# Products of adj_hi first in each half block, four slots of split blocks, eight raw half blocks

## The reference

```
x = layernorm(x + relu(adj @ x @ K + b))            # pass 0
v0 = x, then five applications of adj, each with a three-layer perceptron:
    v = mlp(adj @ u, uv);  u = mlp(adj @ v, vu);  ...   # passes 1 to 5
mlp(x, W1..3, b1..3): leaky_relu(leaky_relu(leaky_relu(x@W1+b1)@W2+b2)@W3+b3), slope 0.01
out = layernorm(x + v)                               # after pass 5
```

## Time and profile before

| | |
|---|---|
| median of three runs | 1184.89 us |
| the profiled execution | 1184.28 us |
| its span, first to last instruction | 1182.5 us |
| mean granted clock of TensorE | 0.997 |
| PE busy | 1157.3 us, 98% |
| DVE busy | 738.1 us, 62% |
| ACT busy | 661.8 us, 56% |
| DMA, mean rate over the span | 221 GB/s |

### The profile page before, as it was taken

How to read it: one execution, slowest core, us unless ns; L and a number is a source line. 1 busy time by engine, 2 the same in 40 slices (tenths; PEclk the granted TensorE clock), 3 DMA queues, 4 the chain that set the end, 5 groups by cost and what they waited for, 6 DMA issues and landing times.

```text
span 1182.5 us, 13669 instructions
## 1 busy us (share of the span) xinstructions
PE 1157.3 (98%) x5220; PEld 951.0 (80%) x5220; DVE 738.1 (62%) x885; ACT 661.8 (56%) x815; POOL 0.2 (0%) x4
## 2 busy tenths in 40 slices
PE   7999999998999999999999999999999999999996
PEld 5777888887888888888888888888888888887775
DVE  7988765458465545665555646544565555668985
ACT  7865544246555545554545645543556544657884
POOL 0000000000000000000000000000000000000000
PEclk9999999999999999999999999999999999999999
DMA  9996766567266556655647635655564656569891
GB/s 363 404 344 237 266 222 218 191 230 251 105 200 208 192 183 209 218 181 193 205 170 247 219 138 177 214 185 190 199 246 159 214 183 227 173 249 348 305 340 45
DMA packets 73073, 261.61 MB, mean 221 GB/s; under 512 B 8112, under 2 KB 8496, under 8 KB 73008
## 3 DMA queue, kind: packets, MB, share of 16 engines
q1 hardware_dynamic: 73008, 260.74, 63.1%
HBM read 258.61 MB, written 2.10 MB: 220 GB/s over the span
## 4 chain that ended last, share of the span: by engine, by line
PE 87%; DMA 6%; DVE 4%; ACT 2%; issue 1%; ACTq 0%; SPq 0%; DVEq 0%
PE agg_ps L646 26%; PE agg_ps L648 26%; PE agg_ps L647 26%; DMA adj_raw<-in_adj 6%; PE pre_ps L678 3%; DVE adj_lo L638 3%; PE hid_ps L646 1%; PE hid_ps L648 1%; PE hid_ps L647 1%; ACT adj_hi L526 1%; PE hid_ps L690 1%; DVE stats L536 0%; ACT resid L448 0%; PE hid_ps L704 0%; ACT hid L427 0%
## 5 line engine op out<-in xcount | busy, mean ns | idle before, releaser
L638 DVE TENSOR_TENSOR adj_lo<-adj_raw,adj_hi 128x1024 fp32r<-128x1024 f32 x488 | 577.9, 1221 | 240.8 <-ACT adj_hi L526 236.8
L646 PE MATMUL agg_ps<-adj_hi,feat_hi 128*128 128x512 f32 x1536 | 610.9, 398 | 11.9 <-DVE adj_lo L638 11.7
L648 PE MATMUL agg_ps<-adj_hi,feat_lo 128*128 128x512 f32 x1536 | 599.7, 390 | 0.0
L647 PE MATMUL agg_ps<-adj_lo,feat_hi 128*128 128x512 f32 x1536 | 599.1, 390 | 0.0
L526 ACT ACTIVATE adj_hi<-adj_raw 128x1024 fp32r<-128x1024 f32 x488 | 492.5, 1052 | 80.1 <-DMA adj_raw<-in_adj 76.7
L646 PEld LDWEIGHTS agg_ps<-adj_hi,feat_hi 128*128 128x128 f32 x1536 | 288.9, 188 | 79.5 <-issue 13.1
L647 PEld LDWEIGHTS agg_ps<-adj_lo,feat_hi 128*128 128x128 f32 x1536 | 289.2, 188 | 61.0 <-issue 3.4
L648 PEld LDWEIGHTS agg_ps<-adj_hi,feat_lo 128*128 128x128 f32 x1536 | 288.8, 188 | 61.2
L427 ACT ACTIVATE hid<-hid_ps,params 128x512 f32<-128x512 f32 (+1 forms) x80 | 54.4, 681 | 78.2 <-PE hid_ps L648 64.1
L492 ACT ACTIVATE in_hi<-part 128x512 fp32r<-128x512 f32 x24 | 15.2, 634 | 103.2 <-DVE part L627 103.2
L427 ACT ACTIVATE post<-pre 128x512 f32<-128x512 f32 (+1 forms) x41 | 25.3, 620 | 80.9 <-DVE pre L607 80.4
(11 more groups left out here) (52 smaller groups left out, 261.7 us busy)
## 6 DMA issues: line engine op xcount, KB each, us to landing
adj_raw<-in_adj SPq DMA_DIRECT2D x488, 512.0 KB, 5.7
resid<-in_x SPq DMA_DIRECT2D x8, 256.0 KB, 6.3
out<-resid SPq DMA_DIRECT2D x7, 256.0 KB, 5.1
params<-in_weights SPq DMA_DIRECT2D x1, 450.0 KB, 6.8
out<-resid SPq DMA_DIRECT2D x2, 128.0 KB, 1.7
b_row<-in_bias_rows SPq DMA_DIRECT2D x1, 192.0 KB, 8.0
```

The source lines that it names most:

```text
L638: dve.tensor_tensor(adj_lo[:, plan.slot[b], slot], adj_raw[:, h % RAW, 0:pieces * CHUNK], adj_hi[:, plan.slot[b], slot].bitcast(F32), ALU. ...
L646: pe.matmul(to, l_hi, r_hi, start=start, stop=False)
L647: pe.matmul(to, l_hi, r_lo, start=False, stop=False)
L648: return pe.matmul(to, l_lo, r_hi, start=False, stop=stop)
```

## The change

In each half block the products with `adj_hi` come first, for both ticks (feat_hi and feat_lo), and the two with `adj_lo` after them; PE waits for `adj_hi` before the first and for `adj_lo` only before the last two. Feature parts are waited for in the same way (hi before the first, lo before the second matmul). There are 4 slots for split blocks and 8 raw half blocks. The order of pass 0 below the top row is written out as one list, `FIRST`. The GCN weight and its bias (64 KB each as stored on the chip) are loaded at load 42 and the rest at load 90; the weights are split at tick 320. TURN does `act_hid1` at 5 in place of 7 and `dve_hid` at 4 in place of 6. The last pass gets faster step tables (LATE2, LATE), its rows end with 3, 1, 2 in place of 3, 2, 1, and the last unit writes its result before the normalisation into a free place of `part`, so it need not wait for the unit before.

```
-RING = 5
-RAW = 6
+RING = 4
+RAW = 8
...
-FIRST_CORNER = (("finish", 0, (2,)), ("finish", 1, (2,)), ...
+FIRST = (("finish", 0, (6,)), ("finish", 1, (6,)), ("finish", 0, (7, 4)), ("finish", 2, (6, 7)),
+         ("finish", 1, (7,)), ("finish", 0, (5,)), ("finish", 1, (5,)), ("finish", 0, (2,)),
+         ("finish", 2, (3, 4, 2)), ("finish", 1, (4,)), ("finish", 3, (5,)), ("finish", 0, (3,)),
+         ("finish", 1, (3, 2)), ("finish", 0, (1, 0)), ("finish", 2, (1,)), ("finish", 1, (0,)),
+         ("finish", 3, (6,)), ("finish", 2, (5,)), ("finish", 1, (1,)), ("begin", 1, (0,)), ("both", 2, (0,)),
+         ("finish", 3, (4,)), ("begin", 2, (1,)), ("finish", 3, (3, 7)), ("finish", 4, (0,)), ("both", 3, (0,)),
...
+         ("finish", 6, (7, 6)), ("both", 6, (0, 1, 2, 3, 4, 5)))
...
-LOAD_PARAMS = 42
-W_SPLIT = 120
+LOAD_GCN, LOAD_PARAMS = 42, 90
+W_SPLIT = 320
...
-    TURN: dict(dve_sum=0, act_in=0, dve_in=0, pe_hid1=4, act_hid1=7, dve_hid=6, pe_hid2=9, act_hid2=11,
+    TURN: dict(dve_sum=0, act_in=0, dve_in=0, pe_hid1=4, act_hid1=5, dve_hid=4, pe_hid2=9, act_hid2=11,
...
-    LATE: dict(dve_sum=0, act_in=0, pe_hid1=2, act_hid1=2, pe_hid2=4, act_hid2=5, pe_out=6, dve_pre=8,
-               act_post=8, dve_stats=10, act_std=12, dve_shift=13, act_norm=14),
+    LATE2: dict(dve_sum=0, act_in=1, pe_hid1=4, act_hid1=5, pe_hid2=6, act_hid2=7, pe_out=8, dve_pre=10,
+                act_post=10, dve_stats=12, act_std=14, dve_shift=15, act_norm=16),
+    LATE: dict(dve_sum=0, act_in=1, pe_hid1=1, act_hid1=1, pe_hid2=2, act_hid2=4, pe_out=4, dve_pre=6,
+               act_post=6, dve_stats=7, act_std=7, dve_shift=8, act_norm=9),
...
+LAST_ROWS = (6, 5, 4, 3, 1, 2)
...
+                if h == LOAD_GCN:
+                    sp.dma_start(params[:, 0:P], weights[:, 0:P]).then_inc(gcn_loaded, 16)
+                    sp.dma_start(b_row[:, 0:P], bias_rows[0:P].partition_broadcast(P)).then_inc(gcn_loaded, 16)
...
+                pe.matmul(group_bank(g), feat_hi[feats][:, tile(src, i)], adj_hi[:, plan.slot[b], piece(i)],
+                          start=start, stop=False)
+                if i == 0 and b in plan.brings_x and s == 0 and into == FINISH:
+                    pe.wait_ge(x_lo_ready, plan.xs.index(c) + 1)
+                if made > n_feats:
+                    pe.wait_ge(feat_lo_ready, made)
+                    n_feats = made
+                pe.matmul(group_bank(g), feat_lo[feats][:, tile(src, i)], adj_hi[:, plan.slot[b], piece(i)],
+                          start=False, stop=False)
                 if i % 2 == 1:
+                    if h > h_lo:
+                        h_lo = h
+                        pe.wait_ge(adj_lo_ready, h + 1)
+                    for k in (i - 1, i):
+                        last = pe.matmul(group_bank(g), feat_hi[feats][:, tile(src, k)],
+                                         adj_lo[:, plan.slot[b], piece(k)], start=False, stop=stop and k == i)
                     last.then_inc(half_used, 1)
```

More of the change, by code:

```diff
@@ L80, in block_products @@
         if s == 0:
[L81 to L84, removed]
+            for what, r, columns in FIRST:
                 yield from dict(finish=finish, begin=begin, both=both)[what](s, r, columns)
[L86 to L89, removed]
         else:
@@ L110, in block_products @@
     yield from finish(s, top, (0,))
-    for r in range(top - 1, 0, -1):
+    for r in LAST_ROWS:
         yield from finish(s, r, range(r, -1, -1))
@@ L217, in steps_of, with on_vector @@
             after = len(self.units) - len(END_UNITS) - u
-            return END if after <= 0 else LATE if after == 1 else LAST
+            return END if after <= 0 else LATE if after == 1 else LATE2 if after == 2 else LAST
         return TURN if r in (0, self.rows - 1) else IN_PARTS
+    def on_vector(self, u):
+        return "dve_norm" in STEPS[self.steps_of(u)]
     def in_parts(self, u):
@@ L397, in norms, with normed_by, wait_for_normed, post_of @@
             return u if u < C else u - LAST_0 + C
+        def normed_by(u, vector):
+            return sum(kind_of(i) in (GCN, LAST) and plan.on_vector(i) == vector for i in range(u + 1))
+        def wait_for_normed(engine, u):
+            if u >= LAST_0:
+                if normed_by(u, True) > C:
+                    engine.wait_ge(dve_normed, normed_by(u, True))
+                if normed_by(u, False):
+                    engine.wait_ge(act_normed, normed_by(u, False))
+        def post_of(u):
+            if plan.steps_of(u) == END:
+                return part_of(chunk_of(plan.first_of(u) - 1))
+            return post
         def at(t, step, kinds):
@@ L465, in _ @@
                     act.wait_ge(pre_ready, u + 1)
-                    if ends(u):
-                        act.wait_ge(out_ready, ends(plan.first_of(u)))
-                    prelu(post[:, own(u)], pre[:, own(u)]).then_inc(post_ready, 1)
+                    if plan.steps_of(u) != END:
+                        wait_for_normed(act, u - 1)
+                    prelu(post_of(u)[:, own(u)], pre[:, own(u)]).then_inc(post_ready, 1)
                 u = at(t, "act_hid2", DEEP)
@@ L535, in statistics @@
                 for j in tiles_of(u):
-                    last = dve.bn_stats(stats[:, j, :], post[:, j * P:(j + 1) * P])
+                    last = dve.bn_stats(stats[:, j, :], post_of(u)[:, j * P:(j + 1) * P])
                 last.then_inc(stats_ready, 1)
@@ L572, in _ @@
                     dve.wait_ge(std_ready, norms(u) + 1)
-                    if ends(u):
-                        dve.wait_ge(out_ready, ends(plan.first_of(u)))
+                    wait_for_normed(dve, plan.first_of(u) - 1)
                     dve.reciprocal(rstd[:, tiles], std[:, tiles]).then_inc(rstd_ready, 1)
@@ L588, in _ @@
                     dve.wait_ge(post_ready, deep(u) + 1)
-                    dve.tensor_tensor(post[:, own(u)], post[:, own(u)], resid[:, columns_of(u)], ALU.add)\
+                    dve.tensor_tensor(post_of(u)[:, own(u)], post_of(u)[:, own(u)], resid[:, columns_of(u)], ALU.add)\
                        .then_inc(total_ready, 1)
@@ L689, in _ @@
                     else:
-                        last = pe.matmul(layer_bank(1, u), w_raw[:, w, :], hid1[:, own(u)], start=True, stop=True)
+                        last = pe.matmul(layer_bank(1, u), w_hid[:, w, :], hid1[:, own(u)], start=True, stop=True)
                     last.then_inc(hid2_done, 1)
```

84 lines of the change are left out of this document (47 added, 37 removed).

## The result

The changed kernel takes 1174.75 us (four runs, 1174.59 to 1175.07), the kernel before beside it 1184.99 us; the ratio is 0.9918, 95% interval 0.9903 to 0.9933. A later set of six runs gave 0.9925 (0.9912 to 0.9938). The change makes the kernel about 0.8% faster. The profiled execution of the changed kernel took 1174.89 us with a span of 1173.1 us.

A forecast was written before the change was run, and what follows sets the result against it. PE bounds the kernel, and its 4608 matmuls (1046 us) don't move. Gains of 4.5 (first stage), 2.9 (turn), 0.3 (later passes) and 0.6 (tail) sum to 8.3 us: 1176.6 us, range 1171.5 to 1182.5.

The forecast's parts named there:

- Up to the first begin: Start of pass 0: parameters moved off load 42, chunks closing sooner and fewer waits gain 4.5 us by tick 108.
- The new stalls behind DVE: Before tick 100: PE stalls some 3.7 us, mostly at loads 45 and 47, behind a unit's statistics and normalisation.
- DVE's queue: Before tick 100: eight splits of 1.15 us and a unit's 4.4 us keep DVE busy until 82.0 us.
- Hi first: In the paced start: two matmuls instead of six remain after adj_lo arrives, 0.9 us once, counted within the first stage.
- The first matmul: At the start: with adj_hi alone it begins near 6.1 us, 1.3 us sooner, but that gain isn't kept.
- The clock: First stage: the new stall could bring the low clock back, costing 0 to 1.7 us; taken as 0.
- The turn: Near 290 us: two splits instead of four before hid_hi, so the wait for hid_lo goes; gain 2.9 us.
- Four slots, eight raw halves: Whole kernel: splits after pass 0 due almost as before, slots free sooner, loads further ahead; taken as 0.
- Passes 1 to 4: Later turns: waits for hid_lo like the first turn's go, gain 0.3 us; the passes otherwise keep their length.
- The last pass: Pass 5: no cost from the buffers, with PE idle under 1 us.
- the rival C: Pass 5: four slots make splits wait, 2.7 us a unit, 1187.5 us with half the cost; chance 0.07.
- The tail: After the last product: gain 1.0 us from earlier steps, less 0.3 to 0.4 of new wait; sum 0.6 us.

The follow-up runs named there:

- after_again: The changed kernel unaltered, measured again in a later set of six runs: 1174.60 us, 0.9925 of the kernel before.
- b_turn: The kernel before with only the new TURN table (act_hid1 5 for 7, dve_hid 4 for 6): 1181.50 us, ratio 0.9973.
- a_ring5: The changed kernel with five slots and six raw half blocks again: 1179.23 us, 0.9970 of the kernel before.
- b_slots: The kernel before with only the four slots and eight raw half blocks: 1186.85 us, ratio 1.0021.
- a_mm_order: The changed kernel with the old order of the matmuls and their waits in each tick: 1176.75 us, 0.9947 of the kernel before.
- a_old_last: The changed kernel with the old LATE table, no LATE2 and last rows 3, 2, 1: 1175.70 us, 0.9936 of the kernel before.
- a_raw6: The changed kernel with six raw half blocks in place of eight, four slots kept: 1178.61 us, 0.9958 of the kernel before.
- a_later_raw10: The changed kernel with later layer steps in TURN, LAST and LATE2 and ten raw half blocks: 1173.07 us, 0.9911 of the kernel before.

## Why the prediction was right

It said 1176.6 us, 8.3 less; measured were 10.2 us less by the medians of those runs, 9.4 by the two profiles. The two large terms, the first stage and the first turn, were right in place and size. The four smaller ones were not: what the buffers do was put at nothing, and a gain of 1.4 us more in the passes 1 to 4 and a loss of 1.1 in the last one nearly cancel, which is luck. Point by point, against the profiles:

- **Up to the first begin**, forecast 4.5: measured 5.0 at the 4th point, 4.1 with after_again. Some of it is the profile that stands for the kernel before: b_turn has the same pass 0, its clock didn't fall, and its 4th point is at 122.4; against that one the stage gives 3.9 or 3.0 us. Tick 100 began at 82.3 (forecast: 82.5) and tick 108 at 88.6 (88.8). Load 42's split by ACT ran from 66.32 to 67.38 (forecast: done at 67.7), but ACT waited only 0.13 us before it, not 1, and tick 84 began at 68.8, not 67.8: PE was busy up to there without a wait that the trace marks since 35 us, with the first unit's `pre_ps` (at 67.0) in front, which the forecast had left out. So DVE's count decided, as forecast. The new stalls behind DVE are there, at the loads before which the unit's statistics and normalisation stand. Forecast were 3.7 us in all, measured 2.3 between starts, of which the trace marks 1.07 and 0.73 as waits:

```profile
75.04 0.74 PE L790 MATMUL agg_ps<-adj_lo,feat_hi 128*128 128x512 f32 x2 [1.07 <-DVE adj_lo L673]
...
78.84 0.74 PE L790 MATMUL agg_ps<-adj_lo,feat_hi 128*128 128x512 f32 x2 [0.73 <-DVE adj_lo L673]
```

- **DVE's queue** shows the forecast order and its durations: the pre, the post and statistics, one split each between, then `resid` at 76.53 and `feat_lo`, which ends at 80.5 (forecast: 80.8, one split before the 82.0 of load 49):

```profile
70.13 0.68 DVE L642 TENSOR_TENSOR pre<-pre_ps,b_row 128x512 f32<-128x512 f32 x1
...
73.79 1.19 DVE L673 TENSOR_TENSOR adj_lo<-adj_raw,adj_hi 128x1024 fp32r<-128x1024 f32 x1
...
76.53 1.11 DVE L586 TENSOR_SCALAR resid<-post,mean_var,rstd 128x128 f32<-128x128 f32 x4
...
79.84 0.68 DVE L600 TENSOR_TENSOR feat_lo<-resid,feat_hi 128x512 fp32r<-128x512 f32 x1
80.44 5.97 DVE L673 TENSOR_TENSOR adj_lo<-adj_raw,adj_hi 128x1024 fp32r<-128x1024 f32 x5
```

- **Hi first**: 0.9 us once, forecast; undoing it costs 2.2 by the medians. The step that I left out is `feat_lo`. In the kernel before the first product after a unit began 0.12 us late and was stretched by another 0.11, once in each pass 1 to 4, and with hi first that is gone: undoing it costs 1.0 us from the 9th to the 40th point.
- **The first matmul** came at 6.98, not at 6.1. It cost nothing that shows, since the loads pace what follows. With the old order of pass 0 it came at 5.97, so it is the list that delays it. ACT waited for the first half block until 5.78, in place of 4.77; with the list SyncE sends the second chunk of x behind four half blocks, with the old order behind six. Whether that is the reason isn't shown.
- **The clock**: I took 0 for a return of the low level, and it stayed at 1.00 in the changed kernel up to the last product. Its new stalls are two of about 1 us with work between them.
- **The turn**, forecast 2.9: measured 2.8 from the 8th to the 9th point. Two splits stand ahead of `hid_hi` instead of four, as forecast:

```profile
280.15 1.99 ACT L561 ACTIVATE adj_hi<-adj_raw 128x1024 fp32r<-128x1024 f32 x2
283.68 0.69 ACT L462 ACTIVATE hid_hi<-hid_ps,params 128x512 fp32r<-128x512 f32 x1 [1.54 <-PE hid_ps L683]
```

  But it takes table and slots together. The prediction has the next two splits due at 384 and 386; the plan with four slots has them at 386 and 388. With five slots and the new table there are three (b_turn 0.73 us of wait, a_ring5 1.47), with four slots and the old table three, too, the last one waiting for its slot (b_slots 1.22). The 0.77 us before it stayed, as forecast.
- **Four slots, eight raw halves: forecast 0.** This is the step that failed. Undone together they cost 2.8 to 3.6 us by the profiles and 4.6 by the medians. Six raw halves in place of eight cost 2.2 us in the first stage, which I had put down as paced by DMA at share 1.03; a share near 1 didn't mean that loads could not be issued sooner to advantage. That holds beside the rest of the change only: in the kernel before, the same buffers brought the 4th point no further. They cost 2.5 us in the last pass, too, with four slots. The four slots cost 1.2 us a pass through ACT's queue beside the old TURN table, which my count of due times missed, because I compared the due times with each other and not with what stands behind a waiting split. The new TURN table takes exactly this away, and beside it the four slots are a gain, since they keep the third split behind `hid_hi`. In the sum all this is hidden, as it is part of what I had booked under the first stage and the turn.
- **Passes 1 to 4**, forecast 0.3: measured 1.7. The TURN table gives 0.7 of it (b_turn, from the 9th to the 40th point; the trace of the kernel before marks 0.29 there as a wait for `hid_lo`), and `feat_lo` the other 1.0 (a_mm_order).
- **The last pass**, forecast 0: 1.1 us worse. With the old buffers it takes 0.8 us less (a_ring5), with the old order of the matmuls 0.3 less (a_mm_order), with the old tables 0.1 less (a_old_last). In the kernel before the buffers alone cost 0.5 us there (b_slots). Of the two buffers it is the slots: a_ring5 and a_raw6 both have six raw halves, and with four slots the pass is 3.3 us longer. One trace of it: the wait of 0.35 us in L745 for DVE's `part` (L704 in the kernel before) stands in every profile with four slots but a_later_raw10, which does that layer a tick later, and in none with five. So the rival C had the sign and the place, at 0.8 us for the pass where it priced 2.7 us a unit.
- **The tail**, forecast 0.6: measured 1.0; with the old tables 0.6 of it is gone.

The parts don't add up one by one. Alone in the kernel before, the four parts tried give -1.5 (parameters), -3.2 (TURN), +0.4 (hi first) and +2.5 us (buffers), -1.8 in all; the change gives 9.4 to 10.2. Of these only TURN and the buffers are clear of noise. Undone alone from the changed kernel, hi first, buffers, list and last tables cost 2.2, 4.6, 2.3 and 1.1 us by the medians; the parameters and the TURN table weren't undone alone. Where the traces show why, a part moves a wait from one engine's queue to the next, and time comes off only where that queue is cleared too: slots and TURN table are the case that was run in all its four forms. What the interplay of list, buffers and hi first in the first stage is in detail wasn't taken apart further.

## What to carry to other kernels

With queues in order, a buffer count isn't neutral because the due times stay the same: look at which instruction stands behind the one that waits for the buffer, and move the urgent one ahead of it before taking a slot away. Judge a part of a change by undoing it in the full version as well as by doing it alone; here the same edit was worth 2.2 us one way and nothing the other. And where PE waits for the result of a layer by less than a tick, let the layer's matmul come one tick later: the next product fills the gap (0.5 us at the turn and 1.3 in the last pass, though with ten raw halves, which weren't tried apart).

## What the runs showed of the hardware

The clock's fall doesn't follow the length of the idle time alone. In the kernel before it fell after 1.80 us of idle time and not after 2.74; with the parameters moved it fell after 2.58 us at that same place, and with hi first alone both after 2.39 us and after 3.17. Each fall cost 1.7 to 1.8 us of work. In the two profiles of the changed kernel, where no wait after the start is above 1.15 us, it didn't fall before the last product (behind it the granted clock is near 0.5 in the changed kernel and in the kernel before alike, with next to no matmul left). The spread of the changed kernel's runs is 1.2 us, that of the kernel before beside after_again 6 us; among those, the runs with a mean clock of 0.995 to 0.996 took 1183.7 to 1186.8 us and those with 0.998 took 1180.8 to 1184.5. The clock isn't all of the spread: the runs of a_raw6 spread over 4.0 us at 0.998 to 0.999. The Trainium skill (TensorE: Matmul & The Clock Gate, Part 1) names idle time as what throttles; the traces agree that each fall came behind a wait, and add that the same wait need not bring one.

Matmul starts were 0.227 us apart in both orders of the three products, although hi first moves the same `adj_hi` piece through twice in a row. The stretch from the 4th to the 8th point, 145.1 us in every profile, shows it to 0.01 us: the order alone is free.
